# Causal mask of the transposed scores: from mask products on TensorE to a select on GpSimd

## What is computed

```python
Q = _rope(split_heads(x @ W_q.T), pos)
K = _rope(split_heads(x @ W_k.T), pos)
V = split_heads(x @ W_v.T)
score = jnp.einsum('bnqd,bnkd->bnqk', Q, K) / jnp.sqrt(jnp.float32(D_K))
causal = jnp.triu(jnp.ones((s, s), dtype=bool), k=1)
score = jnp.where(causal[None, None], -jnp.inf, score)
attn = jax.nn.softmax(score, axis=-1)
out = jnp.einsum('bnqk,bnkd->bnqd', attn, V)
```

## Time and profile before

| | |
|---|---|
| Times of three runs | 982.06, 983.47, 987.12 us |
| Median | 983.47 us |
| Span of the profiled execution | 1048.8 us |
| Attention stage in the profiled execution | about 75 to 650 us |
| Experts and final sums | about 650 to 1049 us |

### The profile page before, as it was taken

The page is one execution under the profiler, slowest core; times in us unless marked ns, Lnnn a source line. Parts: engine busy times, 40 slices in busy tenths (PEclk is TensorE's granted clock), DMA queues, the critical chain, the costliest instruction groups (busy, mean ns, idle before and its releaser), DMA issues.

```text
span 1048.8 us, 20609 instructions
## 1 busy us (share of the span) xinstructions
PE 852.6 (81%) x6580; PEld 615.2 (59%) x6580; DVE 652.3 (62%) x1914; ACT 456.3 (44%) x763; POOL 426.7 (41%) x408
## 2 busy tenths in 40 slices
PE   4569798987987987987987877978977799989955
PEld 3436374664664663664654545757865588867722
DVE  5577658687687687687586674533642233687916
ACT  2115454544544544544543555425433355544410
POOL 3222113135335335335213234374565555664621
PEclk9759898997897897997987998889999999998978
DMA  4685726236336336336395212453545566997783
GB/s 161 147 222 144 216 64 163 75 98 174 98 99 173 99 99 173 98 81 172 98 322 159 85 47 92 144 167 93 166 150 161 161 178 164 383 314 281 247 339 128
DMA packets 89175, 168.72 MB, mean 161 GB/s; under 512 B 14704, under 2 KB 56688, under 8 KB 88816
## 3 DMA queue, kind: packets, MB, share of 16 engines
q1 hardware_dynamic: 75248, 128.85, 42.1%
q0 software_dynamic: 13824, 38.55, 9.9%
HBM read 90.15 MB, written 76.68 MB: 159 GB/s over the span
## 4 chain that ended last, share of the span: by engine, by line
PE 40%; DVE 23%; issue 11%; SPq 8%; DMA 6%; another core or an unknown queue 5%; ACT 4%; POOL 3%; DVEq 0%; ACTq 0%; POOLq 0%
DVE nmax L829 8%; PE ring L1536 6%; PE ring L1314 5%; PE ring L1316 4%; PE ring L1315 4%; PE ring L1392 3%; PE ring L1557 3%; PE ring L1358 2%; SPq L628 2%; PE ring L1383 2%; SPq L629 2%; DMA xg<-sorted_rows 2%; PE ring L1436 2%; PE ring L1522 2%
## 5 line engine op out<-in xcount | busy, mean ns | idle before, releaser
L1244 ACT ACTIVATE prob<-ring 128x1024 f32<-128x1024 f32 (+1 forms) x192 | 167.5, 881 | 215.5 <-PE ring L1383 196.5
L829 DVE TENSOR_REDUCE nmax<-ring 128x2 f32<-128x1024 f32 (+3 forms) x256 | 201.8, 819 | 73.3 <-PE ring L1365 43.6
L736 POOL DMA_INDIRECT expert_rows<-ys,dest x160 | 159.2, 995 | 127.0 <-ACT ys L1198 74.8
L728 POOL DMA_INDIRECT sorted_rows<-xr,idx_all x128 | 130.5, 1019 | 104.8 <-DVE xr L991 71.5
L1536 PE MATMUL ring<-we,xh 128*128 x640 | 160.3, 396 | 0.0
L1536 PEld LDWEIGHTS ring<-we,xh 128*128 128x128 f32 x640 | 121.6, 200 | 14.6
L1054 DVE SCALAR_TENSOR_TENSOR sl<-sl,got,ring 128x128 f32<-128x128 f32 x160 | 48.3, 343 | 109.8 <-ACT sl L1296 62.5
L1358 PE MATMUL ring<-k_st,q_st 48*128 48x512 f32 (+3 forms) x512 | 88.9, 387 | 26.0 <-issue 9.7
L1392 PE MATMUL ring<-prob,v_sb 128*32 128x512 f32 (+3 forms) x1024 | 106.3, 518 | 3.2 <-ACT prob L1244 3.2
L1377 PE MATMUL ring<-maskt_b,halves_b 64*128 64x128 bf16 (+2 forms) x768 | 58.4, 233 | 50.7 <-DVE nmax L829 23.5
L1377 PEld LDWEIGHTS ring<-maskt_b,halves_b 64*128 64x128 bf16 x768 | 22.8, 97 | 125.4 <-issue 56.7
(11 more groups left out here) (203 smaller groups left out, 1650.8 us busy)
## 6 DMA issues: line engine op xcount, KB each, us to landing
xg<-sorted_rows SPq DMA_DIRECT2D x160, 134.0 KB
parts<-part SPq DMA_DIRECT2D x32, 512.0 KB
ykt<-expert_rows SPq DMA_DIRECT2D x14, 1024.0 KB
k_st<-parts SPq DMA_DIRECT2D x64, 128.0 KB
q_st<-parts SPq DMA_DIRECT2D x64, 128.0 KB
we<-w_exp SPq DMA_DIRECT2D x1, 6144.0 KB
sorted_rows<-zeros SPq DMA_DIRECT2D x2, 2144.0 KB, 9.6
sorted_rows<-zeros SPq DMA_DIRECT2D x32, 134.0 KB
```

Source lines behind the costliest of these rows:

```text
L728: pool.indirect_dma_start(out=xs[group_of(s)], out_offset=bass.IndirectOffsetOnAxis(ap=idx_all[:, s, t, k:k + 1], axis=0), in_=xr[:, s % 2 ...
L736: pool.indirect_dma_start(out=yk, out_offset=bass.IndirectOffsetOnAxis(ap=dest[:, j % 8, b:b + 1], axis=0), in_=ys[:, j % NYS, b, :], in_o ...
L829: dve.tensor_reduce(nmax[:, Q % 2, :, pp, qb], slot[:, :, col:col + (qb + 1) * P], AX.X, ALU.max, negate=True).then_inc(s_max, 1)
L1244: act_e.activation(prob[:, u % 2, 2 * half:2 * half + 2, 0:width], slot[:, :, 0:width], ACT.Exp, scale=SCALE).then_inc(s_exp, 1)
```

## The change

The four mask products of every `ST` step are gone, and with them the constant `maskt_b`; the first score product starts the accumulation. The exponentials of masked entries in the diagonal blocks are thus whatever the unmasked score gives. GpSimd gets a new step at every `ST` place of the plan, `cut`: it waits for the exponentials of that half and writes zero over the masked entries, by one `affine_select` in place for each diagonal block (2 heads x 128 columns on 128 partitions). That is 1, 2 and 1 instructions for the halves of units 0, 1 and 2, 8 for a quad, 256 in all. `AV` now waits for the last of them (`s_causal`) in place of the exponentials (`s_exp`). The ring slot is still released by the exponentials. `S` steps keep their mask products.

```diff
+CUT_DONE = running("ST", ST_PARTS)
...
-        maskt_b = place("maskt_b", [P, 2, P], bf16)
...
+        s_causal = sem("exponentials_cut")
...
+            def cut(Q, half, m):
+
+                u = UNITS * Q + m
+                pool.wait_ge(s_exp, ST_DONE[Q, half, m])
+                for kb, col in ST_PARTS[m]:
+                    diagonal = prob[:, u % 2, 2 * half:2 * half + 2, col:col + P]
+                    pool.affine_select(diagonal, diagonal, pattern=[[0, 2], [1, P]], compare_op=ALU.is_ge, fill=0.0, base=0,
+                                       channel_multiplier=-1).then_inc(s_causal, 1)
+
...
+                elif kind == "ST":
+                    cut(n, st[2], st[3])
...
-            for made, col in ((halves_b, K_HALVES), (mask_b, K_MASK), (maskt_b, K_MASKT)):
+            for made, col in ((halves_b, K_HALVES), (mask_b, K_MASK)):
...
                 parts = ST_PARTS[m]
-                diagonal = [col // P for kb, col in parts]
-                for h in range(2):
-                    for par in range(2):
-                        r = slice(64 * par, 64 * par + 64)
-                        mask = maskt_b[r, h, 0:64 * (h + 1)].unsqueeze(1).to_broadcast([64, len(parts), 64 * (h + 1)])
-                        pe.matmul(blocks_of(slot[:, par, :], diagonal)[:, :, 0:64 * (h + 1)], halves_b[r, h, :], mask,
-                                  start=h == 0, stop=False, skip_group_check=True)
-                for kb, col in parts:
+                for n, (kb, col) in enumerate(parts):
                     k0, width = kb * P, T - kb * P
                     for par in range(2):
                         r = slice(64 * par, 64 * par + MROWS)
                         last = pe.matmul(slot[:, par, col:col + width], k_st[r, Q % NQ, half, k0:k0 + P],
-                                         q_st[r, Q % NQ, half, k0:T], start=False, stop=True, skip_group_check=True)
+                                         q_st[r, Q % NQ, half, k0:T], start=n == 0, stop=True, skip_group_check=True)
                 last.then_inc(s_ST, 1)
...
-                    pe.wait_ge(s_exp, ST_DONE[n, 1, m])
+                    pe.wait_ge(s_causal, CUT_DONE[n, 1, m])
```

More of the change, by code:

```diff
@@ L661, in _ @@
             sp.dma_start(stage[:, C_O:], w_small[:, C_O:]).then_inc(s_small, 16)
-            sp.wait_ge(s_init, 8)
+            sp.wait_ge(s_init, 7)
             for st in PLAN:
@@ L749, in _ @@
             pool.memset(v_sb[:, :, :, :, DH:DH + 1], 1.0).then_inc(s_vone, 1)
-            pool.wait_ge(s_init, 8)
+            pool.wait_ge(s_init, 7)
             for st in PLAN:
@@ L1438, in sum_results @@
                 last.then_inc(s_cp, 1)
-            pe.wait_ge(s_init, 8)
+            pe.wait_ge(s_init, 7)
             for st in PLAN:
```

## The result

The changed kernel takes **1014.66 us** (median of 4 runs, 1011.56 to 1016.03) against 983.85 for the kernel before beside it (982.06 to 987.12): 1.031 times, with a 95% interval of 1.028 to 1.034, some 31 us slower. The forecast was slower, 993.5, with a range of 976 to 1014: the sign is right, the size is a third of what came (10 of 31 us), and the time lies just outside the range. The profiled execution of the changed kernel has a span of 1009.8 us.

What follows compares the result with a forecast made beforehand. No single engine was taken as the bound: TensorE and VectorE wait for each other in turn. The terms -5 + 9.8 + 4.7 + 0.5 = +10 us, added unscaled to the median 983.5, gave 993.5 us, range 976 to 1014.

Steps and rivals of the forecast that it cites:

- -5: Gain in us from removing 768 mask products on TensorE in the attention stage, by chain share; bounds 0 and -15.4.
- 9.8: Loss in us from late value products at B: five sequences at 1.4 and one at 2.8; bounds 0 and 16.8.
- 4.7: Loss in us at the last sequence: a value product 6.6 us late makes the transposes behind it start 4.7 late.
- 0.5: Loss in us added for the first sequences, whose GpSimd queue holds only rotary work.
- rival 4: Shared SBUF access: selects lengthen seven of eight L871 residual sums by 0.87 us, 6 us more, about 1000; chance 0.05.
- the cover behind B: A 3.68 us pause right behind B that might absorb its lateness; half was taken, 1.4 us in five sequences.
- B: Value product of unit 1, next quad, at a middle sequence: 2.8 us late behind GpSimd's queue, on the chain.
- unseen releaser: Chain waits whose releaser the profile doesn't show: 4.4% of the chain, one such piece in each of five sequences.
- the clock: TensorE's low clock after a pause at A: 0.5 to 0.9 us in six sequences, 3 to 5 us, outside the sum.
- A: Value product of unit 2 at a middle sequence: 2.95 us late, at most 1.75 going on; one backlog with B.
- Rivals 1 and 2: First: pause hides B, about 981, chance 0.23. Second: also the full 15.4 us gain counts, 971, chance 0.12.
- Rival 3: Full backlog, B counting wholly: select of 0.65 us, 1012, chance 0.14; fixed cost of 1.04 us, 1036, chance 0.06.

Runs made afterwards that it cites:

- a tiny step: Changed kernel with each select replaced by a memset of one element per partition, the value product waiting for it: 992.77 us, ratio 1.009 against the kernel before.
- the quiet quads: Selects only in quads 4s and 4s+3 of the first seven sequences, mask products in all others: 986.60 us, ratio 1.002 against the kernel before.

## Why the prediction was right and wrong

**The step that failed: the selects' own load on GpSimd was put at nothing.** The sum -5 + 9.8 + 4.7 + 0.5 prices only the wait of the value products and the gain on TensorE. That more work on GpSimd holds up VectorE stands in the prediction as rival 4, with 0.05 and 6 us, and among the signs of being wrong, but no term of the sum has it. With the selects made and nobody waiting for them the kernel is 23.3 us slower. The waiting, for which the sum had 15 us, is worth 6.4 when it is taken out of the changed kernel and 7.9 when it is put in by a tiny step. So the largest part of the loss was missing from the sum, and the part that was in it was priced at about twice its worth.

**Right: the price of a select and the places of the waits.** 0.43 us for 0.5, and waits of 2.2 to 2.9 us at unit 2 of quad 4s+1 in five of six sequences, and of 1.6 to 2.0 us at unit 1 of quad 4s+2 in five of six, for 2.95 and 2.8. Laying the new queue over the old timelines found them. In the last sequence it had 6.6 us for one value product, and the longest wait is 2.08.

**Wrong: "I take half, 1.4 us", the cover behind B.** The cover was the pause of the unseen releaser in the earlier trace rows. It was read from an execution whose span was 65 us over the median of the timed runs, and the sum went on from there "unscaled". The repeated profile has none of these pauses. The gap of 65 us was known, and the question it asks (what is in this execution that the timed ones lack?) was not put. That the cover wasn't there doesn't make B count in full, though. In the kernel before, TensorE already waits for VectorE's maxima in front of the counterpart of B (2.60 us, shown above), and its waits of that kind fell from 27.7 to 10.1 us when those for the selects came (31.8).

**Wrong: "-5 us" for the masks.** The time per group was of the right order (0.05 and 0.077 for 0.07 and 0.10), and the gain is none, in two pairs of runs: without any mask the ratio is 1.004, and the change with and without mask products differs by 0.5 us. The step from a share of the chain to a gain failed here. What came is the end 0 of that term.

**A sum that closes by luck.** With the prediction's own bounds, 0 for the masks and 16.8 for B, the sum is 22 us, and with 7.6 for `ve` 29.6, for 31 measured. The runs don't bear this out: they give all waits together 6 to 8 us, and the load 23.3, of which `ve` is 7.6 and the rest stays open. Candidates for the rest are `xr`, `pr`, `r_sf` and `r_g`, which are held but weren't taken out one by one, and the later powers, for which VectorE waits 3.0 us more.

**Wrong: rival 4's size, and its instruction.** It was priced from the residual sum L871 with its two inputs. That sum is not longer after (1.24 us in the mean, 1.34 before). Held were small instructions from SBUF to SBUF: with one tensor input `ve` at 1.27 us for 0.17, `xr` and `pr`, and with two `r_sf` (0.61 for 0.23 in the mean). VectorE's busy time rose by 16.5 us in the stage, `ve` costs about 7.6 of the time, and it stands on the chain right before the power and the selects of place B.

The Trainium skill ("SBUF — State Buffer", section "SBUF: two separate sides") names as what contends with a GpSimd instruction for the shared port pair either a VectorE operation with two SBUF inputs or a "DVE op in a 2-port perf mode", and the loser blocks for the whole instruction. The prediction weighed the first half only, and under it falls `r_sf`, 1.47 us for 0.22 at its longest. If a small fp32 operation such as `ve` runs in such a mode, it is held by the second half. No run shows its mode; that `ve` ends with the low part in both timelines agrees. In these runs it is up to 1.4 us for one `ve`.

**Half right: the clock.** It was left out of the sum and put at 3 to 5 us in six sequences for the group after A. There the eight matmuls of unit 2 took 1.08 us for 0.64 and those of unit 0 behind them 1.77 for 1.06, and in the last sequence 1.93 for 1.07. With the select elsewhere, where no value product waits, these are as short as before, and the kernel is 6.4 us faster than the changed one; how much of that is clock and how much waiting wasn't separated.

**The rivals.** Rivals 1 and 2 are excluded by the time. Rival 3's select of 0.65 us is excluded by the 0.43 measured, and that B counts wholly isn't shown. Its 1012 is close by luck, for it too has only waits in its sum.

## What to carry to other kernels

Ask of a step that goes to a half idle engine not only who waits for it, but whom that engine holds up while it runs: here the load without any waiter cost 23 us, the waiting 6 to 8. Small SBUF-to-SBUF instructions of VectorE are the ones to look at, by whether their end coincides with the end of a GpSimd instruction; and held time is a lead, not a price, since 6.0 us of it in the quiet quads came with 2.4 us of loss. And before a gap in a profile is used as cover, compare the span with the timed runs; if it is longer by several per cent, take another profile first.

## What the runs showed of the hardware

- A VectorE tensor_scalar on 128x4 fp32 from SBUF to SBUF takes 0.17 us alone and up to 1.6 us if a GpSimd sum of two 128x512 inputs runs; the two end together. Being held, 24 such instructions cost the kernel 7.6 us, uncertain by some 5. A tensor_tensor on 128x64 with two SBUF inputs took 1.47 us for 0.22 the same way. Reductions from PSUM were not longer.
- A GpSimd affine select of 256 fp32 per partition takes 0.40 us at least, 0.43 in the mean, between its memset of one element (0.10) and its power of 4 elements (1.04).
- 768 matmuls that filled TensorE's time between other groups could be removed without any gain; the granted clock in the stage was 0.88 without them and 0.91 with them.
- 16 matmuls of 384 columns took 1.93 us at a granted clock of 0.50 and 1.07 us at 1.00. Behind a pause of 2.75 us the clock was 0.50, behind one of 0.84 us 1.00; in the last sequence it was at 0.50 from 607.9 us on, before the pause of 2.08 us and behind it.
